# Copies of the k, v and r projections out of PSUM: from ScalarE to VectorE, in an RWKV layer with a gated FFN

## The chip, the cores and the metric

The kernel runs on all 8 cores of one Trainium2 chip. Each core takes one of the 8 sequences of the batch (4096 tokens of 1024 features), with no exchange between cores. The time is device microseconds of the slowest core.

## What is computed

```python
xn = layer_norm(x, ln1_w, ln1_b)
lx = time_shift(xn)
k = (xn * time_mix_k + lx * (1.0 - time_mix_k)) @ w_key
v = (xn * time_mix_v + lx * (1.0 - time_mix_v)) @ w_value
r = (xn * time_mix_r + lx * (1.0 - time_mix_r)) @ w_recept
out = wkv(exp(time_decay), time_first, k, v)      # a scan over the 4096 tokens
x = x + out * sigmoid(r) @ w_output
...
# channel mix: relu(fk)^2 @ f_w_value, gated by sigmoid(fr); then layer norm,
# then silu(x @ wg.T) * (x @ wu.T) @ wd.T with int weights / 127, and layer norm
```

Only the first lines, up to k, v and r, are computed in the part of the program that the change touches.

## The kernel before

The program runs in stages with a barrier of all engines behind each of them: the first computes k, v and r and leaves them in DRAM, the second does the scan, and the later ones do the channel mix and the FFN. The change is in the first stage alone.

That stage is a loop over 8 blocks of 512 tokens, followed by one more call of `emit_projA`. What one turn i emits, in this order:

- SyncE loads the block of x (L406) into one of two buffers.
- The layer norm: VectorE sums (L291, four of 1024 columns), ScalarE sums squares (L297), ScalarE and GpSimd pass small statistics to each other (L301 to L325), and ScalarE applies them (L412).
- TensorE transposes the block in 8 groups (L350). Each group fills a PSUM bank, which ScalarE copies into `xn` (L421).
- VectorE mixes the block with its shifted self: for each of 8 chunks one difference (L427) and three mixes into `m_k`, `m_v`, `m_r` (L434). These have two buffers each, by the parity of i. GpSimd then keeps the last column (L441).
- For i of 1 and more, `emit_projA(i - 1)`: the projections of the block of the turn before. For k, v and r, and for each twice, TensorE does four tiles of 128x512 (L340, 32 matmuls) into four of the 8 PSUM banks, four copies bring them into the four staging tiles of that name (L392), and ScalarE's queue issues four stores of 256 KB to DRAM (L396). Below, k1 and k2 are the first and second group of four of k, and so for v and r.
- GpSimd converts an eighth of the FFN's integer weights with DMAs alone: a load with conversion (L280) and a store (L283), through a single staging tile.

There is no scheduler. Each engine runs its instructions in the order in which the Python emits them, and `Builder.op` adds waits on semaphores from what is read and written. Two of its rules matter. A store names the whole DRAM tensor as what it writes, so each store of `k_fm` waits until the one before has landed. And a group of copies waits until the stores that read the same four staging tiles have landed, which for k2 are those of k1.

Of the kernel before, what the change touches and what calls it, by code (L numbers as in the profile page):

```python
# [9 lines left out]
AF = mybir.ActivationFunctionType  # L10
# [170 lines left out]
def build(debug_phases=99, debug_outs=()):  # L181
# [48 lines left out]
    B = Builder(nc)  # L230
    for s in B.all_sems():
# [17 lines left out]
        reads=[ident], writes=[ident])  # L249
# [4 lines left out]
    for p, h in pv_h.items():  # L254
# [4 lines left out]
         reads=[P["tdec"]], writes=[dw])  # L259
    B.op("scalar", lambda e: e.activation(dw.ap, dw.ap, AF.Exp, scale=-1.0),  # L260
         reads=[dw], writes=[dw])
    B.op("scalar", lambda e: e.activation(eu.ap, P["tfir"].ap, AF.Exp),
         reads=[P["tfir"]], writes=[eu])
# [105 lines left out]
    for w_h, w_sb in ((wk_h, wk_sb), (wv_h, wv_sb), (wr_h, wr_sb)):  # L369
        B.op("gpsimd", lambda e, w_h=w_h, w_sb=w_sb: e.dma_start(  # L370
            w_sb.ap, w_h.rearrange("(c p) o -> p c o", p=128)),
            writes=[w_sb], dma=True)
    B.op("gpsimd", lambda e: e.memset(xn.ap[:, :, 0:1], 0.0), writes=[xn])

    def emit_projA(i):
        t0 = 512 * i
        m_k, m_v, m_r = m_k2[i % 2], m_v2[i % 2], m_r2[i % 2]
        for name, w_sb, m, dst, hb in (("k", wk_sb, m_k, k_fm, HB["k_fm"]),
                                       ("v", wv_sb, m_v, v_fm, HB["v_fm"]),
                                       ("r", wr_sb, m_r, r_fm, HB["r_fm"])):  # L380
            for ob in range(0, DC, 4):
                jobs = []
                for oc in range(ob, ob + 4):
                    pb = pool.take()
                    jobs.append((pb, [w_sb.ap[:, kc, oc * 128:(oc + 1) * 128] for kc in range(DC)],
                                 [m.ap[:, kc, :] for kc in range(DC)]))
                mm_jobs(jobs, 512, [w_sb, m])
                sgs = [stg[name][oc % 4] for oc in range(ob, ob + 4)]

                def evac4(e, jobs=jobs, sgs=sgs):  # L390
                    for k4 in range(4):
                        e.activation(sgs[k4].ap, jobs[k4][0].ap, AF.Copy)  # L392
                    return e.nop()
                B.op("scalar", evac4, reads=[j[0] for j in jobs], writes=sgs)
                for k4, oc in enumerate(range(ob, ob + 4)):
                    B.op("scalar", lambda e, dst=dst, oc=oc, t0=t0, sg_=sgs[k4]: e.dma_start(  # L396
                        dst[oc * 128:(oc + 1) * 128, t0:t0 + 512], sg_.ap),
                        reads=[sgs[k4]], writes=[hb], dma=True)

    if debug_phases >= 1:  # L400
        for i in range(8):
# [6 lines left out]
                writes=[x_t], dma=True)  # L408
# [8 lines left out]
            for dc in range(DC):  # L417
# [7 lines left out]
                    reads=[pb, P["ln1w"], P["ln1b"]], writes=[xn])  # L425
            for dc in range(DC):
# [3 lines left out]
                    reads=[xn], writes=[dnc])  # L430

                def mixes(e, dc=dc, m_k=m_k, m_v=m_v, m_r=m_r):
                    for tm, m in (("tmk", m_k), ("tmv", m_v), ("tmr", m_r)):
# [5 lines left out]
                     reads=[dnc, xn, P["tmk"], P["tmv"], P["tmr"]],  # L439
                     writes=[m_k, m_v, m_r])  # L440
            B.op("gpsimd", lambda e: e.tensor_copy(xn.ap[:, :, 0:1], xn.ap[:, :, 512:513]),  # L441
                 reads=[xn], writes=[xn])
# [23 lines left out]
    if debug_phases >= 2:  # L466
        for j in range(DC):
            kb, vb, rb = kb2[j % 2], vb2[j % 2], rb2[j % 2]
            yb, kmax = yb2[j % 2], kmax2[j % 2]
            for src, hb, b in ((k_fm, HB["k_fm"], kb), (v_fm, HB["v_fm"], vb),  # L470
# [3 lines left out]
                    reads=[hb], writes=[b], dma=True)  # L474
            if j == 7 and "dbg" in debug_outs:
                B.op("sync", lambda e: e.dma_start(dbg_h[:, 0:4096], rb.ap),
                     reads=[rb], dma=True)
# [6 lines left out]
                reads=[kmax], writes=[kmax])  # L484
            B.op("vector", lambda e, kmax=kmax: e.tensor_scalar(
                kmax.ap[:, 1:2], kmax.ap[:, 1:2], 20.0, None, ALU.min),
                reads=[kmax], writes=[kmax])
            B.op("scalar", lambda e, kb=kb, kmax=kmax: e.activation(
                ek.ap, kb.ap, AF.Exp, bias=kmax.ap[:, 1:2]),
                reads=[kb, kmax], writes=[ek])  # L490
            B.op("vector", lambda e, vb=vb: e.scalar_tensor_tensor(
                ekv.ap, ek.ap, 1.0, vb.ap, ALU.mult, ALU.mult),
                reads=[ek, vb], writes=[ekv])
# [3 lines left out]
                reads=[ekv, dw], writes=[Abuf])  # L497
# [3 lines left out]
                reads=[ek, dw], writes=[Bbuf])  # L501
# [3 lines left out]
                reads=[ekv, eu, Abuf], writes=[kb])  # L505
# [3 lines left out]
                reads=[ek, eu, Bbuf], writes=[vb])  # L509
            B.op("vector", lambda e, vb=vb: e.scalar_tensor_tensor(  # L510
                ekv.ap, tmp.ap, 1.0, vb.ap, ALU.add, ALU.mult),
                reads=[tmp, vb], writes=[ekv])
# [4 lines left out]
            if j == 7 and "dbg" in debug_outs:  # L517
                B.op("sync", lambda e: e.dma_start(dbg_h[:, 4096:8192], Abuf.ap[:, 0:4096]),
                     reads=[Abuf], dma=True)
                B.op("sync", lambda e: e.dma_start(dbg_h[:, 8192:12288], kb.ap),  # L520
                     reads=[kb], dma=True)
                B.op("sync", lambda e: e.dma_start(dbg_h[:, 12288:12290], kmax.ap),
                     reads=[kmax], dma=True)
# [5 lines left out]
                reads=[kb, tmp], writes=[yb])  # L529
            B.op("scalar", lambda e, j=j, yb=yb: e.dma_start(  # L530
                y_fm[j * 128:(j + 1) * 128, :], yb.ap),
                reads=[yb], writes=[HB["y_fm"]], dma=True)
# [21 lines left out]
    if debug_phases >= 3:  # L554
        for w_h, w_sb in ((wo_h, wo_sb), (fwk_h, fwk_sb), (fwr_h, fwr_sb)):
            B.op("gpsimd", lambda e, w_h=w_h, w_sb=w_sb: e.dma_start(
                w_sb.ap, w_h.rearrange("(c p) o -> p c o", p=128)),
                writes=[w_sb], dma=True)
# [40 lines left out]
        for i in range(16):  # L599
# [6 lines left out]
                writes=[xc], dma=True)  # L606
            B.op("sync", lambda e, t0=t0, yc=yc: e.dma_start(
                yc.ap, y_fm.rearrange("(c p) t -> p c t", p=128)[:, :, t0:t0 + 256]),
                reads=[HB["y_fm"]], writes=[yc], dma=True)
# [292 lines left out]
```

How the kernel before makes its waits and increments, by code:

```python
    def _wait(self, eng, tok):  # L58
        sem, val, src, flag = tok
        prev = self.waited[eng].get(sem.name, -1)
        if val <= prev:
            return
        self.waited[eng][sem.name] = val
        flag["x"] = True
        self.ops[eng].append(lambda e, s=sem, v=val: e.wait_ge(s.h, v))
# [33 lines left out]
            def fn(e, build=build, sem=sem, step=step):  # L99
                ins = build(e)
                ins.then_inc(sem.h, step)
# [1 line left out]
            def fn(e, build=build, sem=sem, step=step, flag=flag):  # L103
                ins = build(e)
                if flag["x"]:
                    e.drain().then_inc(sem.h, step)
                else:
                    ins.then_inc(sem.h, step)
# [72 lines left out]
def build(debug_phases=99, debug_outs=()):  # L181
# [648 lines left out]
                                 bias=stat.ap[:, 24 + q:25 + q],  # L830
                                 scale=stat.ap[:, 20 + q:21 + q])
                return e.nop()
            B.op("scalar", napplyD, reads=[y2p, stat], writes=[y1tc])
            B.op("sync", lambda e, t0=t0: e.dma_start(
                out_h[t0:t0 + 512, :].rearrange("(q p) d -> p q d", p=128), y1tc.ap),
                reads=[y1tc], dma=True)
    ar.release()
    for ds in B.dsems["sync"] + B.dsems["scalar"]:
        B.raw("sync", lambda e, ds=ds: e.wait_ge(ds.h, ds.n))
    for ds in B.dsems["gpsimd"]:
        B.raw("gpsimd", lambda e, ds=ds: e.wait_ge(ds.h, ds.n))
```

## Time and profile before

| | us |
|---|---|
| two runs of the kernel before | 5155.95 and 5321.26, median 5238.6 |
| the profiled execution's own time | 5163.81 |
| its span, on the slowest core (core 5) | 5162.3 |
| spans of the other cores | 5100.2 to 5147.8 |

The span is from the first instruction to the last on the slowest core, and the time of the execution lies 1.5 us above it. The rows below are of that execution and that core. A row of the timeline gives an instruction's start and duration in us, and in square brackets how long its engine was idle before it and who released it. A merged row (x4) has the duration from the first start to the last end.

### The profile page before, as it was taken

The page shows a single profiled execution, that of the slowest core. Times are in us where ns is not written, and L with a number is a line of the kernel's source. Part 1 is how long each engine was busy: PE and PEld are TensorE (multiplying, and loading weights), DVE is VectorE, ACT ScalarE, POOL GpSimd, SP SyncE. Part 2 cuts the span into 40 slices and gives each one's busy share as a digit, 9 for nine tenths or more (in the row PEclk, how much of TensorE's full clock was granted, in tenths as well). Part 3 has the DMA queues.
Part 4 walks back from the last instruction along what each step waited for, and adds up shares of the span by engine and source line. Part 5 has one row for each costly group of instructions (what it writes and reads, how often), then busy time and mean ns, then how long its engine had stood idle before and what let it go on. Part 6 is the DMA issues. An engine that isn't in the chain of part 4 may idle for free.

```text
span 5162.3 us, 42328 instructions; the slowest of 8 cores (5100.2 to 5162.3 us)
## 1 busy us (share of the span) xinstructions
PE 2882.8 (56%) x14080; PEld 1451.6 (28%) x14080; DVE 1338.4 (26%) x1840; ACT 981.0 (19%) x1414; POOL 145.7 (3%) x328
## 2 busy tenths in 40 slices
PE   0445655400004777777762767764599999155554
PEld 0112222100002444455441323332244444022222
DVE  2222321067742444334430111211011111010101
ACT  1123222122212222232220111121011111011101
POOL 1100000000000000000000000000000000000000
PEclk9966777755556888888886878877799999577777
DMA  6333334533244122221217243233310110413132
GB/s 106 100 108 110 108 100 116 157 143 141 114 94 106 62 82 82 62 82 62 70 50 175 82 135 110 84 128 78 61 66 33 55 44 25 114 57 114 57 114 73
DMA packets 351011, 472.55 MB, mean 92 GB/s; under 512 B 83536, under 2 KB 263760, under 8 KB 345680
## 3 DMA queue, kind: packets, MB, share of 16 engines
q1 hardware_dynamic: 111488, 218.11, 12.8%
q10 hardware_dynamic: 215552, 186.67, 11.1%
q0 software_dynamic: 23760, 65.07, 7.0%
q8 instruction: 119, 1.95, 0.2%
q14 instruction: 92, 0.75, 0.1%
HBM read 293.65 MB, written 203.42 MB: 96 GB/s over the span
## 4 chain that ended last, share of the span: by engine, by line
issue 28%; PEld 20%; DMA 17%; DVE 10%; ACT 7%; DVEq 5%; ACTq 5%; PEldq 4%; another core or an unknown queue 2%; POOLq 1%; POOL 0%; SPq 0%
PEld psum L340 18%; DVEq L106 5%; ACTq L106 4%; PEldq L106 4%; DMA v_fm<-arena 3%; DMA r_fm<-arena 3%; DMA k_fm<-arena 2%; DMA arena<-h_fm 2%; DMA arena<-wd_bf 2%; ACT arena L297 2%; PEld psum L350 2%; POOLq L106 1%; DVE arena L498 1%; DVE arena L494 1%
## 5 line engine op out<-in xcount | busy, mean ns | idle before, releaser
L340 PE MATMUL psum<-arena 128*128 128x512 bf16 (+1 forms) x13312 | 2686.8, 364 | 1548.3 <-DMA arena<-x 529.5
L340 PEld LDWEIGHTS psum<-arena 128*128 128x128 bf16 x13312 | 1333.7, 102 | 2896.5 <-issue 1864.6
L350 PE MATMUL psum<-arena 128*128 128x128 f32 x768 | 196.0, 386 | 702.1 <-ACTq L106 655.7
L297 ACT ACTIVATE arena<-arena 128x1024 f32<-128x1024 f32 x128 | 133.6, 1045 | 1764.7 <-DVEq L106 1487.5
L350 PEld LDWEIGHTS psum<-arena 128*128 128x128 f32 x768 | 117.8, 192 | 784.7 <-issue 784.7
L778 DVE SCALAR_TENSOR_TENSOR arena<-psum,arena 128x512 bf16<-128x512 f32 x192 | 123.7, 686 | 728.3 <-ACTq L106 728.3
L574 DVE TENSOR_SCALAR arena<-psum 128x256 f32<-128x256 f32 x512 | 181.3, 416 | 383.6 <-PEq L106 235.1
L772 ACT ACTIVATE arena<-psum 128x512 bf16<-128x512 f32 x192 | 104.2, 594 | 610.7 <-PEq L106 604.3
L705 DVE SCALAR_TENSOR_TENSOR arena<-psum,arena 128x512 f32<-128x512 f32 x64 | 44.2, 691 | 671.0 <-PEq L106 664.7
L821 DVE SCALAR_TENSOR_TENSOR arena<-psum,arena 128x512 f32<-128x512 f32 x64 | 44.3, 692 | 664.2 <-PEq L106 655.2
L427 DVE SCALAR_TENSOR_TENSOR arena<-arena 128x512 f32<-128x512 f32 x64 | 44.3, 692 | 614.0 <-ACTq L106 602.7
L578 ACT ACTIVATE arena<-arena 128x1024 bf16<-128x1024 f32 x128 | 135.3, 1057 | 334.9 <-DVEq L106 328.9
L392 ACT ACTIVATE arena<-psum 128x512 f32<-128x512 f32 x192 | 99.1, 602 | 517.0 <-DMA v_fm<-arena 163.7
L291 DVE TENSOR_REDUCE arena<-arena 128x1 f32<-128x1024 f32 x128 | 147.9, 1212 | 24.0 <-DMA arena<-x 15.5
L434 DVE SCALAR_TENSOR_TENSOR arena<-arena 128x512 bf16<-128x512 f32 x192 | 132.9, 747 | 15.1 <-DVEq L106 15.1
L652 DVE SCALAR_TENSOR_TENSOR arena<-arena 128x256 f32<-128x256 f32 x128 | 54.5, 426 | 299.9 <-ACTq L106 277.7
L658 DVE SCALAR_TENSOR_TENSOR arena<-arena 128x256 bf16<-128x256 f32 x256 | 112.7, 481 | 25.4 <-DVEq L106 25.4
L513 ACT ACTIVATE arena<-arena 128x4096 f32<-128x4096 f32 x8 | 28.9, 3616 | 292.3 <-DVEq L106 292.3
L311 POOL TENSOR_TENSOR arena<-arena 128x4 f32<-128x4 f32 (+1 forms) x40 | 7.8, 196 | 2678.9 <-ACTq L106 2630.4
L646 ACT ACTIVATE arena<-psum,arena 128x256 f32<-128x256 f32 x128 | 72.4, 565 | 35.3 <-ACTq L106 20.4
L494 DVE TENSOR_TENSOR_SCAN arena<-arena 128x4096 f32<-128x4096 f32 x8 | 69.5, 8693 | 1.6 <-DVEq L106 1.6
L498 DVE TENSOR_TENSOR_SCAN arena<-arena 128x4096 f32<-128x4096 f32 x8 | 69.5, 8693 | 1.0 <-issue 0.2
(75 smaller groups left out, 879.5 us busy)
## 6 DMA issues: line engine op xcount, KB each, us to landing
fk_fm<-arena ACTq DMA_DIRECT2D x16, 2048.0 KB, 8.8
arena<-fk_fm SPq DMA_DIRECT2D x8, 4096.0 KB, 25.1
h_fm<-arena ACTq DMA_DIRECT2D x8, 3072.0 KB, 11.1
arena<-h_fm SPq DMA_DIRECT2D x8, 3072.0 KB, 16.2
arena<-x SPq DMA_DIRECT2D x8, 2048.0 KB, 9.6
k_fm<-arena ACTq DMA_DIRECT2D x64, 256.0 KB, 2.2
v_fm<-arena ACTq DMA_DIRECT2D x64, 256.0 KB, 2.6
r_fm<-arena ACTq DMA_DIRECT2D x64, 256.0 KB, 2.4
```

Of the source, the lines that this page charges most:

```text
L106: e.drain().then_inc(sem.h, step)
L291: e.reduce_sum(stat.ap[:, q:q + 1], xa[:, q, :], AX.X)
L297: e.activation(dump.ap[:, q, :], xa[:, q, :], AF.Square, accum_out=stat.ap[:, 4 + q:5 + q])
L340: last = e.matmul(psumb.ap[:, 0:n], lts[i], rhs[i], start=(i == 0), stop=(i == cnt - 1))
L350: last = e.transpose(bank.ap[:, idx * 128:(idx + 1) * 128], ap, ident.ap)
L434: e.scalar_tensor_tensor(m.ap[:, dc, :], dnc.ap, P[tm].ap[:, dc:dc + 1], xn.ap[:, dc, 0:512], ALU.mult, ALU.add)
L494: B.op("vector", lambda e, j=j: e.tensor_tensor_scan(Abuf.ap[:, 1:4097], dw.ap[:, j:j + 1].to_broadcast([128, 4096]), ekv.ap, 0.0, ALU.mul ...
L498: B.op("vector", lambda e, j=j: e.tensor_tensor_scan(Bbuf.ap[:, 1:4097], dw.ap[:, j:j + 1].to_broadcast([128, 4096]), ek.ap, 0.0, ALU.mult ...
L574: e.tensor_scalar(relu_t.ap[:, k4 * 256:(k4 + 1) * 256], jobs[k4][0].ap[:, 0:256], 0.0, None, ALU.max)
L578: B.op("scalar", lambda e, fb=fb, fkst=fkst: e.activation(fkst.ap[:, fb:fb + 4, :].rearrange("p a b -> p (a b)"), relu_t.ap, AF.Square), r ...
L658: e.scalar_tensor_tensor(m.ap[:, dc, :], dn2.ap, P[tm].ap[:, dc:dc + 1], xn2.ap[:, dc, 0:256], ALU.mult, ALU.add)
L778: e.scalar_tensor_tensor(hbv.ap[:, hc, :], jobs[2 + k2][0].ap, 1.0, sgb.ap[:, hc, :], ALU.mult, ALU.mult)
```

## The change

The four copies of each group are done by VectorE as `tensor_copy`, where ScalarE did them as `activation` with the function Copy. The stores stay in ScalarE's queue, and nothing else is edited.

```diff
@@ -389,9 +389,9 @@
 
                 def evac4(e, jobs=jobs, sgs=sgs):
                     for k4 in range(4):
-                        e.activation(sgs[k4].ap, jobs[k4][0].ap, AF.Copy)
+                        e.tensor_copy(sgs[k4].ap, jobs[k4][0].ap)
                     return e.nop()
-                B.op("scalar", evac4, reads=[j[0] for j in jobs], writes=sgs)
+                B.op("vector", evac4, reads=[j[0] for j in jobs], writes=sgs)
                 for k4, oc in enumerate(range(ob, ob + 4)):
                     B.op("scalar", lambda e, dst=dst, oc=oc, t0=t0, sg_=sgs[k4]: e.dma_start(
                         dst[oc * 128:(oc + 1) * 128, t0:t0 + 512], sg_.ap),
```

VectorE, from the end of the mixes of turn 1 to the first difference of turn 2, in the kernel before (sem_tensor, sem_scalar, sem_vector and sem_gpsimd are the engines' semaphores, d_sync and d_scalar those of DMAs on these queues):

```order
L427 SCALAR_TENSOR_TENSOR arena<-arena 128x512 [waits sem_vector]
L434 SCALAR_TENSOR_TENSOR arena<-arena 128x512 [waits sem_vector]
L434 SCALAR_TENSOR_TENSOR arena<-arena 128x512 x2
L437 NO_OP
L291 TENSOR_REDUCE arena<-arena 128x1 [waits d_sync2,sem_gpsimd]
L291 TENSOR_REDUCE arena<-arena 128x1 x3
```

And at the same place in the changed kernel, up to the first copies of v:

```order
L427 SCALAR_TENSOR_TENSOR arena<-arena 128x512 [waits sem_vector]
L434 SCALAR_TENSOR_TENSOR arena<-arena 128x512 [waits sem_vector]
L434 SCALAR_TENSOR_TENSOR arena<-arena 128x512 x2
L437 NO_OP
L392 COPY arena<-psum 128x512 [waits sem_tensor]
L392 COPY arena<-psum 128x512 x3
L393 NO_OP
L392 COPY arena<-psum 128x512 [waits sem_tensor,sem_vector,d_scalar0,d_scalar1,d_scalar2,d_scalar3]
L392 COPY arena<-psum 128x512 x3
L393 NO_OP
L392 COPY arena<-psum 128x512 [waits sem_tensor]
```

All 24 copies of a turn now stand behind its last mix and ahead of the sums of the next turn (L291). The second group waits for the four stores of the first.

ScalarE at the same turn, from its last copies into `xn` to the first store of v, in the kernel before:

```order
L421 ACTIVATE arena<-psum,arena 128x512 [waits sem_tensor,sem_scalar] x7
L392 ACTIVATE arena<-psum 128x512 [waits sem_tensor]
L392 ACTIVATE arena<-psum 128x512 x3
L393 NO_OP
L396 DMA k_fm<-arena 128x512 [waits sem_scalar]
L396 DMA k_fm<-arena 128x512 [waits d_scalar0]
L396 DMA k_fm<-arena 128x512 [waits d_scalar1]
L396 DMA k_fm<-arena 128x512 [waits d_scalar2]
L392 ACTIVATE arena<-psum 128x512 [waits sem_tensor,d_scalar3]
```

And in the changed kernel:

```order
L421 ACTIVATE arena<-psum,arena 128x512 [waits sem_tensor,sem_scalar] x7
L396 DMA k_fm<-arena 128x512 [waits sem_vector]
L396 DMA k_fm<-arena 128x512 [waits d_scalar0]
L396 DMA k_fm<-arena 128x512 [waits d_scalar1]
L396 DMA k_fm<-arena 128x512 [waits d_scalar2]
L396 DMA k_fm<-arena 128x512 [waits sem_vector,d_scalar3]
L396 DMA k_fm<-arena 128x512 [waits d_scalar4]
L396 DMA k_fm<-arena 128x512 [waits d_scalar5]
L396 DMA k_fm<-arena 128x512 [waits d_scalar6]
L396 DMA v_fm<-arena 128x512 [waits sem_vector]
```

The 24 stores of a turn follow each other in ScalarE's queue, and the first of each group of four waits for VectorE. TensorE's, GpSimd's and SyncE's instructions stand as before.

## Rows read from the trace of the kernel before

**Rows 1.** The page: span, busy time, and the chain that ended last.

```profile
span 5162.3 us, 42328 instructions; the slowest of 8 cores (5100.2 to 5162.3 us)
PE 2882.8 (56%) x14080; PEld 1451.6 (28%) x14080; DVE 1338.4 (26%) x1840; ACT 981.0 (19%) x1414; POOL 145.7 (3%) x328
issue 28%; PEld 20%; DMA 17%; DVE 10%; ACT 7%; DVEq 5%; ACTq 5%; PEldq 4%; another core or an unknown queue 2%; POOLq 1%; POOL 0%; SPq 0%
```

**Rows 2.** Waits, 60 to 1014 us: total us, times, longest us.

```profile
DVE arena L427 <- ACTq L106: 602.7, 8, 80.3
...
ACT arena L392 <- DMA v_fm<-arena: 163.7, 14, 16.1
ACT arena L392 <- DMA k_fm<-arena: 134.0, 14, 13.0
ACT arena L392 <- DMA r_fm<-arena: 113.4, 9, 19.5
...
ACT arena L297 <- DMA r_fm<-arena: 53.4, 6, 12.0
```

**Rows 3.** Timeline of ScalarE and its queue, turn 4.

```profile
512.74 0.78 ACT L421 ACTIVATE arena<-psum,arena 128x512 f32<-128x512 f32 x1 [0.41 <-PEq L106]
...
525.46 6.67 ACTq L396 DMA_DIRECT2D k_fm<-arena  x4
533.99 2.06 ACT L392 ACTIVATE arena<-psum 128x512 f32<-128x512 f32 x4 [8.67 <-DMA k_fm<-arena]
536.19 6.92 ACTq L396 DMA_DIRECT2D k_fm<-arena  x4
543.21 2.07 ACT L392 ACTIVATE arena<-psum 128x512 f32<-128x512 f32 x4 [7.16 <-DMA k_fm<-arena]
545.42 9.33 ACTq L396 DMA_DIRECT2D v_fm<-arena  x4
...
592.21 1.06 ACT L297 ACTIVATE arena<-arena 128x1024 f32<-128x1024 f32 x1 [8.04 <-DMA r_fm<-arena]
```

**Rows 4.** Timeline of VectorE, turn 4 and the start of turn 5.

```profile
513.72 0.69 DVE L427 SCALAR_TENSOR_TENSOR arena<-arena 128x512 f32<-128x512 f32 x1 [78.83 <-ACTq L106]
...
537.07 2.08 DVE L434 SCALAR_TENSOR_TENSOR arena<-arena 128x512 bf16<-128x512 f32 x3 [0.19 <-DVEq L106]
539.40 4.60 DVE L291 TENSOR_REDUCE arena<-arena 128x1 f32<-128x1024 f32 x4 [0.26 <-issue]
617.42 0.69 DVE L427 SCALAR_TENSOR_TENSOR arena<-arena 128x512 f32<-128x512 f32 x1 [73.42 <-ACTq L106]
```

**Rows 5.** Seven windows from first mix to first k1 store; then to last mix's end.

```profile
sum 81.22, DVE 69.00; mean DVE 9.86
...
sum 178.37, DVE 155.05; mean DVE 22.15
```

**Rows 6.** Lines by form, VectorE; then its timeline in the channel mix stage.

```profile
L574 DVE TENSOR_SCALAR arena<-psum 128x256 f32<-128x256 f32 x512 | 181.3, 416 | 383.6 <-PEq L106 235.1 <-ACTq L106 145.3 <-issue 3.2
L434 DVE SCALAR_TENSOR_TENSOR arena<-arena 128x512 bf16<-128x512 f32 x192 | 132.9, 747 | 15.1 <-DVEq L106 15.1
...
L652 DVE SCALAR_TENSOR_TENSOR arena<-arena 128x256 f32<-128x256 f32 x128 | 54.5, 426 | 299.9 <-ACTq L106 277.7 <-DVEq L106 22.2
...
1801.76 1.42 DVE L574 TENSOR_SCALAR arena<-psum 128x256 f32<-128x256 f32 x4 [2.58 <-PEq L106]
```

**Rows 7.** The page's DMA part for 512 to 593 us: 40 slices, GB/s moved.

```profile
GB/s 0 0 0 0 0 0 8 129 129 129 129 0 129 134 133 134 154 243 129 122 129 252 7 114 145 259 110 159 144 235 17 238 104 235 62 125 186 202 159 184
```

**Rows 8.** Timeline of TensorE, turn 4: k2 and r2.

```profile
524.11 7.07 PE L340 MATMUL psum<-arena 128*128 128x512 bf16 x32 [0.97 <-PEq L106]
...
559.84 8.58 PE L340 MATMUL psum<-arena 128*128 128x512 bf16 x32 [6.44 <-ACTq L106]
```

**Rows 9.** Timeline of GpSimd, turn 4: its first and last weight DMA.

```profile
540.45 0.63 POOL L280 DMA_DIRECT2D arena<-wu  x1 [0.65 <-issue]
...
593.12 0.55 POOL L283 DMA_DIRECT2D wu_bf<-arena  x1 [4.16 <-DMA arena<-wu]
```

## The prediction

> **What bounds the kernel now.** I read the page first. No engine is full: TensorE is busy for 56% of the span, VectorE for 26%, ScalarE for 19%, and the chain that ended last is spread over issue, weight loads and DMAs [rows 1]. So shares say nothing here, and the stage that the change touches has to be read by itself. It ends with a barrier, at about 1014 us of the 5162.3 (where the window of [rows 2] ends), and what it gains or loses is passed on whole.
>
> The waits of that stage name the engine that carries it [rows 2]. VectorE waits 602.7 us for ScalarE in 8 waits, one per turn. ScalarE in turn waits for DMAs that its own queue issued: 163.7, 134.0 and 113.4 us ahead of the copies, 53.4 ahead of the next turn's squares, 464.5 us in 43 waits. The bound is ScalarE's queue, in which 24 stores per turn follow each other one landing at a time.
>
> The timeline of turn 4 shows the pattern [rows 3, 4]. I count from S, the start of the first mix on VectorE (513.72). ScalarE ends the last copy into `xn` at 513.52, waits for TensorE's k1, copies it out and issues the first k1 store at S + 11.7 (525.46). Each four stores take three landings to issue (6.67 us for k1). Then come 2.06 us of copies, and so on, until the squares of the next turn at S + 78.5. VectorE mixes meanwhile, without a pause, until 539.15 (537.07 + 2.08), S + 25.4, and then has nothing on the path until the next turn. So two things run side by side in this kernel: 25 us of mixes, and the first copies and stores.
>
> **The change, part by part.** What is new in the order is that k1's copies stand behind the last mix on the same engine.
>
> 1. The first copies of a turn wait for the mixes. In turns 1 to 7, S to the first store is 81.22 us in sum, 11.60 each, and S to the end of the last mix 178.37 in sum, 25.48 each [rows 5]. In the changed kernel the first store can go out 25.48 + 0.20 (a step within VectorE's queue, as the 0.19 in [rows 4]) + the four copies + 0.20 (a handoff between engines: 513.52 to 513.72 in [rows 3, 4]).
>
> No copy of 128x512 on VectorE is in the trace. The nearest row is a TENSOR_SCALAR out of PSUM, f32 to f32, of half the width: 416 ns alone, and 1.42 us for four, so (1.42 - 0.416) / 3 = 0.335 us from start to start [rows 6]. The 256 columns more come at the rate at which VectorE's two widths of one operation differ, 0.69 us for 512 columns [rows 4] and 0.426 for 256 [rows 6], so 1.03 ns each, 0.267 us. That makes 0.602 from start to start, 0.683 for the last, 3 x 0.602 + 0.683 = 2.49 us for four. From below the bound is 1.42 (if the wider copy cost no more than that row), from above 4 x 0.747 = 2.99, the mixes' own duration [rows 6]. I take 2.49.
>
> First store at 25.48 + 0.20 + 2.49 + 0.20 = S + 28.37 in place of S + 11.60: +16.77 us, times 7 turns = +117.4. In the tail, projections of block 7, no mix stands ahead.
>
> 2. The second group of each name (k2, v2, r2, 24 in all) still waits for the four stores of the first, as its staging tiles are theirs. It was 2.06 us of copies and 0.14 to the store (536.19 - 533.99 = 2.20 [rows 3]) and becomes 2.49 + 0.20 = 2.69: +0.49, times 24 = +11.8.
>
> 3. The first groups of v and r (16), and k1 of the tail (1), lose their place on ScalarE. From the issue of k2's fourth store to v1's first there are now 545.42 - (536.19 + 6.92) = 2.31 us [rows 3]. In the changed kernel VectorE copies v1 out during k2's stores, and v1's first store can go at once, while k2's fourth is still on its way. I take 2.1 for a gain of 2.31, with 0.2 for two stores in flight: 17 x 2.1 = -35.7. The bounds are 2.31 and 0, should the two merely share the DMA engines.
>
> The rate speaks for nearly all of it: while k1's stores land alone 129 GB/s are moved, and where a weight DMA runs beside a store the sum reaches 243 to 259 [rows 7].
>
> The Trainium skill says of a DMA issued by GpSimd (DMA: Bandwidth & Descriptors, Anatomy of one DMA) that about 2.0 us of it are fixed, most of that the receipt of the last write. By that rule two in flight overlap almost wholly, and term 3 would be its full -39.3. The trace agrees in kind only: by the page's figures a store of 256 KB would take an estimated 2.6 us, and k1's here take 6.67 / 3, about 2.2, with their issue [rows 3].
>
> 4. What could be late next. The sums of the next turn (L291, 4.60 us [rows 4]) move behind r2's copies. The squares follow three landings after r2's first store, and start 8.04 us after r2's copies [rows 3], so about 3 us are left and the sums cost nothing. TensorE gets its banks later: v1's matmuls can start once k1 is copied, at S + 28.2. At 7.07 to 8.58 us a group [rows 8] v1 is done by S + 37, and its copies stand behind k2's, which start about S + 37. The weight DMAs on GpSimd start behind the last mix in both kernels and take 53 us [rows 9]: they end at S + 80, before the next statistics at about S + 97. Of the stores' time (S + 12 to S + 78) the last 51 us lay beside them. It will be S + 28 to S + 92, and the first 52 us lie beside them, so the contention hardly changes. I cost these at nothing. The next turn's S follows the squares as before.
>
> The sum: 117.4 + 11.8 - 35.7 = +93.5 us on the execution's own 5163.8: 5257.3, or 1.8% more. This execution is near the lower of the two runs shown (5155.95). The median of the two, 5238.6, lies 75 us above it and is a mean with the high run, so I don't add to it.
>
> One rule goes against the new engine. The half-width row shows no faster mode: 335 ns from start to start for 256 columns, 1.3 ns each with what one instruction costs [rows 6]. The Trainium skill (VectorE: DVE Perf Modes, Why PSUM operands drop a tier) says that a copy of 32-bit data takes two per cycle between SBUF tiles, but one if an operand lies in PSUM; the trace agrees. By the page's cycle table, PSUM to SBUF, four copies would be an estimated 2.63 us, and by two per cycle about 1.6; with the 31 groups that are waited for (7 + 24) that is 4 us more in the sum, or 28 less.
>
> **The rivals.**
>
> Rival A, the loss is larger (slower by over 2%). Two stores in flight share the DMA engines, and term 3 shrinks to 0.5 x 17 = -8.5: 5163.8 + 117.4 + 11.8 - 8.5 = 5284.5. The slices of 129 and 259 GB/s [rows 7] speak against it. It could also come by TensorE, which now pauses 10.7 us ahead of v1 (k2 ends at 531.18, S + 17.5 [rows 8]). If its groups then took twice 7.07, v1, v2, r1 and r2 would end at S + 28.2 + 56.6 = S + 84.8. R2's copies, now at 582.10 or S + 68.4 (592.21 - 8.04 - 2.07 [rows 3]), would be due at 68.4 + 16.8 + 2 x 0.49 - 2 x 2.1 = S + 82.0, so 2.8 us late, and 7 x 2.8 = 20 us more give 5277. R2's group, which followed a pause of 6.44, took 8.58, not 14 [rows 8]. It decides from 10 us above the forecast on.
>
> Rival B, the stores get shorter (not slower). All 43 waits for stores come to 464.5 us [rows 2]; undisturbed, as in k1 and k2 of turn 4, they would be about 24 x 8.67 + 19 x 7.16 = 344 [rows 3]. If the later start took the stores out of the weight DMAs' way, up to 120 us would go: 5257 - 120 = 5137, no slower than before. It decides from 94 us of relief on. But the stores only move with the mixes' end, and the weight DMAs start at that same point [rows 9], so I see no more than noise.
>
> Rival C, the copies are quick. If four cost 1.42 us, 31 groups save 1.07 each: 33 us, 5224. The half-width row [rows 6] speaks against it.
>
> **How the numbers follow.** Forecast with its small errors, between 5230 and 5267: 0.58. Rival A with its two causes: 0.31. Rival C: 0.08. Rival B: 0.03. A measurement of this kernel tells about 2% from no change, so the border is 5267 above and 5061 below. Slower by over 2%: rival A, 0.31. Within 2%: 0.68. Faster by over 2%: 0.01, as even rival B with all its relief doesn't get there. The range takes the bounds of the unknown terms: below, copies of 1.42 and the full 2.31: 5257 - 33 - 4 = 5220; above, copies of 2.99 (31 x 0.50 = 15.5) and no gain in term 3 (35.7): 5308.
>
> **What would show each step.** In the changed profile the first k1 store of turns 1 to 7 should stand 28 us behind the first mix, with copies of about 0.68 us, four in 2.5. The turn should be about 14 us longer and the stage's end, now 1014, near 1107. ScalarE should wait for VectorE once per turn for about 15 us (S to the first store), and v1's and r1's first stores should follow the fourth of the group ahead within 0.5 us. TensorE should stand idle some 10 us before v1. The later stages should be as they were. I am wrong if the first store comes before the mixes end, if the stores' landings differ in the mean by over 0.3 us from now, or if a later stage changes by over 20 us.

## The result, and the profile after

The changed kernel is slower by 2.1%: the ratio of its runs to those of the kernel before is 1.0212, with a 95% interval of 1.0179 to 1.0244. The median is 5283.91 us of 11 runs, against 5175.17 of 10. These medians hold runs in which one die's cores had a lower clock; the ratio leaves those out on both sides. The profiled execution took 5272.66 us, 108.9 more than that of the kernel before (5163.81). The forecast was 5257, +1.8%, with a range of 5220 to 5308. The measured difference is just above the border of 2%, and the interval reaches across it, so whether the loss is over or under 2% stays open; that there is one does not.

The page of the changed kernel, the span, what each engine did, and the group of the copies:

```profile
span 5271.1 us, 42491 instructions; the slowest of 8 cores (5222.0 to 5271.1 us)
...
PE 2891.7 (55%) x14080; PEld 1452.8 (28%) x14080; DVE 1458.3 (28%) x2032; ACT 881.9 (17%) x1222; POOL 145.6 (3%) x328
...
L392 DVE COPY arena<-psum 128x512 f32<-128x512 f32 x192 | 119.2, 683 | 426.9 <-DMA v_fm<-arena 160.1
```

Against [rows 1], ScalarE did 99 us less and VectorE 120 us more. No sum of busy time tells that the kernel lost 109 us by it. A copy takes 683 ns on VectorE in the mean, as forecast.

The timeline of turn 4 on ScalarE and its queue, core 3, answers to [rows 3]:

```profile
547.30 0.78 ACT L421 ACTIVATE arena<-psum,arena 128x512 f32<-128x512 f32 x1 [0.21 <-ACTq L106]
576.66 22.89 ACTq L396 DMA_DIRECT2D k_fm<-arena  x8
599.64 26.67 ACTq L396 DMA_DIRECT2D v_fm<-arena  x8
626.39 20.66 ACTq L396 DMA_DIRECT2D r_fm<-arena  x8
647.21 1.06 ACT L297 ACTIVATE arena<-arena 128x1024 f32<-128x1024 f32 x1 [99.12 <-DMA r_fm<-arena]
```

ScalarE ends its last copy into `xn` at 548.08 and computes nothing for 99 us. For the first 28.6 us of that its queue issues nothing either. The first store is 28.45 us behind the first mix (548.21), where it was 11.74. From there on the stores of one tensor follow those of the other with no gap: the row of k ends at 576.66 + 22.89 = 599.55, and the first v store goes out at 599.64.

The same turn on VectorE answers to [rows 4]:

```profile
548.21 0.69 DVE L427 SCALAR_TENSOR_TENSOR arena<-arena 128x512 f32<-128x512 f32 x1 [27.27 <-ACTq L106]
...
571.52 2.08 DVE L434 SCALAR_TENSOR_TENSOR arena<-arena 128x512 bf16<-128x512 f32 x3 [0.19 <-DVEq L106]
574.06 2.49 DVE L392 COPY arena<-psum 128x512 f32<-128x512 f32 x4 [0.46 <-issue]
588.27 2.48 DVE L392 COPY arena<-psum 128x512 f32<-128x512 f32 x4 [11.72 <-DMA k_fm<-arena]
591.22 2.48 DVE L392 COPY arena<-psum 128x512 f32<-128x512 f32 x4 [0.46 <-issue]
614.10 2.48 DVE L392 COPY arena<-psum 128x512 f32<-128x512 f32 x4 [20.40 <-DMA v_fm<-arena]
...
637.56 2.48 DVE L392 COPY arena<-psum 128x512 f32<-128x512 f32 x4 [18.04 <-DMA r_fm<-arena]
640.30 4.60 DVE L291 TENSOR_REDUCE arena<-arena 128x1 f32<-128x1024 f32 x4 [0.25 <-issue]
```

The copies of k1 start 0.46 us after the last mix. Those of v1 (591.22) come straight behind those of k2, and v1's staging tiles are full at 593.70, 6 us before v's first store. The sums of the next turn end at 644.90, ahead of the squares at 647.21, so they cost nothing.

TensorE in the same turn, core 3, answers to [rows 8]:

```profile
555.36 7.07 PE L340 MATMUL psum<-arena 128*128 128x512 bf16 x32 [0.97 <-PEq L106]
576.73 9.04 PE L340 MATMUL psum<-arena 128*128 128x512 bf16 x32 [14.30 <-DVEq L106]
590.93 8.75 PE L340 MATMUL psum<-arena 128*128 128x512 bf16 x32 [5.17 <-DVEq L106]
```

After k2 it waits 14.30 us until VectorE has emptied k1's banks. V1 is then done at 585.77, before its copies start at 591.22, so the wait costs nothing here.

The seven windows from first mix to first store, as in [rows 5], now for core 3:

```profile
sum 197.06, DVE 172.49; mean DVE 24.64
```

That is 28.15 us each, and it is 28.14 to 28.16 on all eight cores. In the kernel before it was 11.60 on core 5, whose rows the forecast used, but between 10.12 and 11.60 over the cores, 10.71 in the mean. Core 5 was the longest of the eight.

To see where the time went I add up each part over the turns, mean over 8 cores. Block 7 has no turn of mixes behind it; its stores are the tail.

| us | before | after | difference in sum |
|---|---|---|---|
| first mix to first store, 7 turns | 10.71 | 28.15 | +122.1 |
| first to last store's issue, 7 turns | 72.64 | 72.83 | +1.3 |
| last store's issue to next first mix, 6 | 26.13 | 25.79 | -2.0 |
| tail (block 7), with the step into it | 73.8 | 62.0 | -11.8 |
| end of the first stage | 997.2 | 1107.1 | +109.9 |
| all that follows | 4132.6 | 4141.9 | +9.3 |

The stage holds the difference. The rest moved 9 us, and over the two kernels and the three of the next section that keep the weights where they were it lies between 4132 and 4159 us, so that is noise. The end of the stage has a standard deviation over the 8 cores of 11.8 us before and 6.2 after, which leaves the 109.9 uncertain by some 5 us.

The last thing to see is how long a store takes to land. The chain of waits, core 5, turn 4: first the kernel before, where v1's first store is the row at 545.42.

```profile
545.42 2.05 DMA v_fm<-arena
547.53 4.06 DMA v_fm<-arena
551.66 2.70 DMA v_fm<-arena
554.43 3.10 DMA v_fm<-arena
```

Then the changed kernel, where it is the row at 603.86. The two rows ahead are k1's last store and k2's first.

```profile
588.44 3.12 DMA k_fm<-arena
594.30 2.34 DMA k_fm<-arena
...
603.86 5.09 DMA v_fm<-arena
609.01 3.07 DMA v_fm<-arena
612.15 4.59 DMA v_fm<-arena
```

This pair is an extreme one. Over blocks 0 to 5 and the 8 cores v1's first store lands in 4.06 us where it was 3.14, and r1's in 3.75 where it was 2.57. The stores that have a weight DMA beside them land in 2.99 us (18.8 of 24 per turn) where it was 2.85 (18.3 of 24). Nearly all of that rise lies in v1's and r1's first stores: without these two it is 2.88 where it was 2.85. The stores with no weight DMA beside them take 2.10 where they took 2.13.

### The profile page after: what moved, and what is told of

Read it like the earlier page. It is cut to its first block, busy times and chain, and to the rows that moved or that the text cites. A ratio compares the mean times of both kernels' runs of the same rounds, so it can differ in the third digit from the quotient of the medians.

```text
span 5271.1 us, 42491 instructions; the slowest of 8 cores (5222.0 to 5271.1 us)
## 1 busy us (share of the span) xinstructions
PE 2891.7 (55%) x14080; PEld 1452.8 (28%) x14080; DVE 1458.3 (28%) x2032; ACT 881.9 (17%) x1222; POOL 145.6 (3%) x328
## 4 chain that ended last, share of the span: by engine, by line
issue 26%; PEld 19%; DMA 18%; DVE 12%; DVEq 8%; ACT 6%; ACTq 4%; PEldq 4%; another core or an unknown queue 2%; POOLq 1%; POOL 0%; SPq 0%
PEld psum L340 17%; DVEq L106 7%; ACTq L106 4%; DMA v_fm<-arena 3%; DMA k_fm<-arena 3%; PEldq L106 3%; DMA r_fm<-arena 3%; DMA arena<-h_fm 2%; DMA arena<-wd_bf 2%; ACT arena L297 2%; PEld psum L350 1%; POOLq L106 1%; DVE arena L498 1%; DVE arena L494 1%
## 5 line engine op out<-in xcount | busy, mean ns | idle before, releaser
L392 DVE COPY arena<-psum 128x512 f32<-128x512 f32 x192 | 119.2, 683 | 426.9 <-DMA v_fm<-arena 160.1
L291 DVE TENSOR_REDUCE arena<-arena 128x1 f32<-128x1024 f32 x128 | 147.9, 1212 | 19.5 <-DMA arena<-x 10.7
L434 DVE SCALAR_TENSOR_TENSOR arena<-arena 128x512 bf16<-128x512 f32 x192 | 132.9, 748 | 12.7 <-DVEq L106 12.7
L311 POOL TENSOR_TENSOR arena<-arena 128x4 f32<-128x4 f32 (+1 forms) x40 | 7.8, 196 | 2769.6 <-ACTq L106 2722.8
L513 ACT ACTIVATE arena<-arena 128x4096 f32<-128x4096 f32 x8 | 28.9, 3616 | 291.9 <-DVEq L106 291.9
L478 ACT ACTIVATE arena<-arena 128x4096 f32<-128x4096 f32 x8 | 28.9, 3616 | 251.7 <-DMA arena<-r_fm 214.5
L494 DVE TENSOR_TENSOR_SCAN arena<-arena 128x4096 f32<-128x4096 f32 x8 | 69.5, 8693 | 1.6 <-DVEq L106 1.6
```

The lines of the kernel that those rows point to most:

```text
L291: e.reduce_sum(stat.ap[:, q:q + 1], xa[:, q, :], AX.X)
L392: e.tensor_copy(sgs[k4].ap, jobs[k4][0].ap)
L434: e.scalar_tensor_tensor(m.ap[:, dc, :], dnc.ap, P[tm].ap[:, dc:dc + 1], xn.ap[:, dc, 0:512], ALU.mult, ALU.add)
L494: B.op("vector", lambda e, j=j: e.tensor_tensor_scan(Abuf.ap[:, 1:4097], dw.ap[:, j:j + 1].to_broadcast([128, 4096]), ekv.ap, 0.0, ALU.mul ...
```

## The experiments

Eleven kernels were run. The end of the first stage is the last landing of a k, v or r store, the mean over the 8 cores of one profile. Its standard deviation over the cores is 2 to 17 us, called scatter below; how far it would differ between executions was not measured. The change of the whole kernel by each experiment is the ratio to the kernel before.

### Only v1 and r1 on VectorE

```diff
+                on_v = name != "k" and ob == 0
...
-                        e.activation(sgs[k4].ap, jobs[k4][0].ap, AF.Copy)
+                        if on_v:
+                            e.tensor_copy(sgs[k4].ap, jobs[k4][0].ap)
+                        else:
+                            e.activation(sgs[k4].ap, jobs[k4][0].ap, AF.Copy)
...
-                B.op("scalar", evac4, reads=[j[0] for j in jobs], writes=sgs)
+                B.op("vector" if on_v else "scalar", evac4,
+                     reads=[j[0] for j in jobs], writes=sgs)
```

> The kernel before, with only the first copies of v and of r (v1, r1) on VectorE; k1, k2, v2, r2 stay on ScalarE. This is term 3 of the prediction alone. My term as predicted: 2.1 us gained 16 times, 34 us, ratio to before 0.993, end of the first stage (mean over cores, 997 us in the kernel before) at 963. Theory now (the first store of v and of r lands later because the one ahead is still in flight, as 4.06 and 3.75 us after the change against 3.14 and 2.57 before it): 2.31 less about 1.05 gained, 20 us, stage end at 977. Rival, the two stores merely share the DMA engines: nothing gained, stage end at 997.

Measured: ratio 0.9962 (0.9925 to 0.9999), stage end at 986.0 us, 11 us less than before. The ratio stands for 20 us less, with an interval from nothing to 39, so it can't tell the forecast's 34 from a small gain. The profile shows 11, uncertain by 5, between the 20 of the theory and the nothing of the rival. First to last store's issue took 71.13 us a turn, 1.5 less than 72.64, where 2 x 2.1 was forecast. A store landed in 2.92 us in the mean instead of 2.81.

### k back on ScalarE

The same edit with `on_v = name != "k"`: all copies of v and r on VectorE, those of k on ScalarE.

> The changed kernel with k's copies (k1, k2) back on ScalarE, v's and r's on VectorE. Theory (what costs is that the first copies stand behind the mixes, 17.5 us a turn): the first store comes again 10.7 us after the first mix, and the stage ends at about 997 - 20 (v1, r1 hidden) + 7 (v2, r2 slower by 0.46 each) = 984 us, ratio to before 0.997. Rival, VectorE's copies are dear wherever they stand (their duration, the handoff, more contention): two thirds of the 110 us stay, stage end at 1070, ratio 1.014.

Measured: ratio 1.0005 (0.9967 to 1.0044), stage end at 990.9 us. First mix to first store is 10.97 us again. With 16 of the 24 copies of a turn still on VectorE, the stage ends 116 us earlier than in the changed kernel and 6 earlier than in the one before, and the ratio shows no difference to the latter. So for v and r neither the engine nor its copies' duration costs anything that can be measured. What cost was where k's copies stood.

### k1 and k2 in between the mixes

```diff
                      writes=[m_k, m_v, m_r])
+                if i >= 1 and dc == 2:
+                    emit_projA(i - 1, (0,))
+                if i >= 1 and dc == 5:
+                    emit_projA(i - 1, (1,))
...
             if i >= 1:
-                emit_projA(i - 1)
+                emit_projA(i - 1, (2, 3, 4, 5))
```

> The changed kernel, all copies on VectorE, with k1's copies placed behind the third of the eight chunks of mixes and k2's behind the sixth. Theory: first store about 12.8 us after the first mix (28.15 in the changed kernel, 10.7 before), 15.3 us less in each of 7 turns, and the stage ends near 1107 - 107 = 1000 us, ratio to before about 1.001. Rival, ScalarE's queue needs the copies' engine for another reason than order: the stage stays above 1070 us, ratio 1.014 or more.

Measured: ratio 1.0034 (0.9997 to 1.0071), stage end at 1016.7 us, 90 less than the changed kernel. First mix to first store is 12.37 us (12.8 expected). All copies are on VectorE here, as in the changed kernel; only their place differs. The stage ended 17 us later than expected. Part of that is the tail: from block 7's first store to the end it took 70.6 us, and 61.6 in the changed kernel. The last weight DMA is issued 22 us after block 7's first store here, and 8 us before it in the changed kernel, so they run beside it again.

### Without weight DMAs beside the stores

Three kernels in which GpSimd's weight conversion is moved whole into the scan stage: the kernel before, the one with v1 and r1 on VectorE, and the changed one.

```diff
-            emit_ffn_dequant(i / 8.0, (i + 1) / 8.0)
...
+    wstg = [ar.bf16([128, 3072], "wstg0")] * 2
...
     if debug_phases >= 2:
+        emit_ffn_dequant(0.0, 1.0)
         for j in range(DC):
```

> The kernel before with the conversion of the FFN's weights moved whole from the first stage to the scan stage, so that no DMA of GpSimd runs beside the stores of k, v, r. It is the base for the next two. Theory (stores land in 2.81 us in the mean because weight DMAs run beside them, in about 2.18 without them, as in the tail): 192 x 0.63 = 121 us less, the first stage ends at 876 us (mean over cores) in place of 997. If the landings are slow for another reason, it stays near 997.

> The same with v1's and r1's copies on VectorE: term 3 without weight DMAs. Theory (the gain of 2.31 is eaten by weight DMAs that fill the gaps, not by the second store in flight): 2.1 gained 16 times, the first stage 34 us shorter than in the run before it. Rival (two stores in flight share the engines in any case): 11 us shorter, as with the weight DMAs beside them (997.2 to 986.0).

> The changed kernel with the weight conversion moved to the scan stage. Theory: against the first of these three kernels +122 (first copies behind the mixes, 17.45 x 7) + 11 (k2, v2, r2) - 36 (17 x 2.1) = 97 us, near the 93.5 of the prediction. Rival (sharing in any case): 110 us or more, as with the weight DMAs beside them.

Measured, with the time between the first and the last store's issue of a turn, and the mean landing of a store:

| | stage end | against the first | first to last issue | landing |
|---|---|---|---|---|
| kernel before, weights later | 854.5 | | 60.53 | 2.23 |
| v1, r1 on VectorE, weights later | 828.8 | -25.7 | 57.54 | 2.28 |
| changed kernel, weights later | 944.7 | +90.2 | 56.61 | 2.22 |

The first kernel's stage came out 22 us shorter than expected: 41 of its 143 us lie in turn 1, whose first mix starts at 141.6 us in place of 183.1, since its statistics no longer stand behind turn 0's weight DMAs; the shorter landings, 2.23 us in place of 2.81, are enough for the rest.

The change costs 90 us here (97 expected by the theory, 110 or more by the rival) and 110 with the weight DMAs in place. Between the first and last store it now gains 3.9 us a turn (60.53 to 56.61), where with them it lost 0.2. V1 and r1 alone give 26 us, where they gave 11; that lies between the 34 of the theory and the 11 of the rival. The scatters of 10 to 16 us over the cores leave these differences uncertain by 7 to 8 us each, and those with the weight DMAs in place by 5. So the step from 11 to 26 us is within the noise, and that from 110 to 90 just outside of it. What is clear is the stretch between first and last store of the whole change: a gain of 3.9 us a turn, uncertain by 0.8, against a loss of 0.2, uncertain by 0.7. Without weight DMAs the gain is what was forecast or more, and with them it is gone. First mix to first store is 28.15 and 10.96, nearly as with the weight DMAs (28.15 and 10.71). The ratio of the second kernel was 0.9951 (0.9826 to 1.0077); the third has none, as it was run twice.

As a change to the kernel, moving the weights gains nothing (0.9971, 0.9906 to 1.0036): the stage is 143 us shorter and the rest 136 us longer (4269.0 for 4132.6). The scan stage then loads k, v and r beside them; that this is what makes it longer was not tested.

### The stores no longer wait for each other

```diff
-                        reads=[sgs[k4]], writes=[hb], dma=True)
+                        reads=[sgs[k4]], dma=True)
```

> The kernel before with its stores of k, v and r no longer waiting for each other (they write different parts of the tensors; staging tiles and the barrier still guard them). Theory: the bound moves from ScalarE's queue to GpSimd's, where the weight DMAs of a turn (57 us) start behind the last mix and the next statistics stand behind them: a turn of 25.7 + 57 + 20 = 103 us in place of 109.5, and the first stage ends at about 925 us (997 now).

> The changed kernel with the stores unchained in the same way. Theory (the change costs what it does because the stores' chain starts with the first copies; the weight DMAs start behind the mixes in both): within 15 us of the run before it. If the first copies behind the mixes cost by themselves, it is some 110 us longer than that one.

Measured: the first has a ratio of 0.9842 (0.9794 to 0.9891) and its stage ends at 911.4 us; the second's stage ends at 932.5, 21 later in place of 110. It was expected within 15, and 21 is a little more. From first mix to first mix a turn is only 1.2 us longer, 7 us in six turns, as the 17.3 us ahead of the first store are taken out of a wait; the other 14 come in turn 7 and block 7, where nothing hides them. The second has no ratio, as it was run twice. The timeline of GpSimd in the first of them, core 3, shows the wait:

```profile
564.47 0.53 POOL L280 DMA_DIRECT2D arena<-wu  x1 [2.31 <-DMA wu_bf<-arena]
568.83 0.54 POOL L283 DMA_DIRECT2D wu_bf<-arena  x1 [3.83 <-DMA arena<-wu]
569.39 0.21 POOL L311 TENSOR_TENSOR arena<-arena 128x4 f32<-128x4 f32 x1
```

The statistics of the next turn (L311) start 0.02 us behind the last weight DMA's issue, without any wait: they had stood behind it. That weight chain starts at the end of the mixes in both kernels, so where it sets the turn, the change is nearly free.

### Both edits, with the copies on either engine

The stores unchained and the weights moved to the scan stage, with ScalarE's copies and with VectorE's.

> The kernel before with the stores unchained and the weight conversion moved to the scan stage. Theory: TensorE's six groups bound the turn, about 77 us in place of 109.5; the first stage ends at about 704 us, the rest takes 4269 us as when the weights alone were moved: 4973 us, ratio to before 0.965.

> The changed kernel with the same two edits. Theory: copies stand behind the mixes again, and now TensorE waits for the banks until 28 us after the first mix: a turn of about 90 us, the first stage ends near 795 us, 90 longer than in the run before it, ratio to before 0.983. Rival (VectorE's copies relieve ScalarE once stores don't wait): as fast as that one or faster.

Measured: with ScalarE 0.9614 (0.9585 to 0.9644), stage end at 690.4 us; with VectorE 0.9886 (0.9805 to 0.9967), stage end at 806.2 us. The change costs 116 us in this frame, 26 more than expected, and by the wait that was expected, not by the stores' chain. TensorE in the second, core 6:

```profile
326.58 7.07 PE L340 MATMUL psum<-arena 128*128 128x512 bf16 x32 [1.00 <-ACTq L106]
334.62 7.07 PE L340 MATMUL psum<-arena 128*128 128x512 bf16 x32 [0.98 <-PEq L106]
355.19 9.29 PE L340 MATMUL psum<-arena 128*128 128x512 bf16 x32 [13.50 <-DVEq L106]
```

K1 and k2 run, then v1 waits 13.5 us for VectorE to empty k1's banks, behind the mixes. In the changed kernel itself that wait (14.30 us) is there too, and hidden behind the stores' chain. A turn is 17.0 us longer here (74.99 to 91.98 from first mix to first mix), the whole delay of the first copies.

### The weights behind the statistics

Stores unchained, copies on ScalarE, and:

```diff
             ln_stats(x_t, 4, stat, n_t)
+            emit_ffn_dequant(i / 8.0, (i + 1) / 8.0)
...
-            emit_ffn_dequant(i / 8.0, (i + 1) / 8.0)
```

> The kernel before, copies on ScalarE, stores unchained, and the weight DMAs of a turn issued by GpSimd right behind that turn's statistics (ahead of the last-column copy L441) in place of behind the mixes. Theory: the weight stream of 57 us then fits beside TensorE's and ScalarE's work of a turn, the turn stays near the 75 us of the kernel with the weights in the scan stage, and the scan stage is not lengthened: first stage at about 720 us, the rest 4140 us, 4860 us in all, ratio to before 0.942. If the weight stream still holds the next statistics back, the first stage stays above 850 us.

Measured: ratio 0.9462 (0.942 to 0.9504), the stage ends at 715.0 us and the rest takes 4138.7. This beats both kernels, by 5.4% and about 7.3%. GpSimd's timeline, core 6:

```profile
353.73 0.55 POOL L283 DMA_DIRECT2D wu_bf<-arena  x1 [3.95 <-DMA arena<-wu]
354.79 0.20 POOL L442 COPY arena<-arena 128x8 f32<-128x8 f32 x1 [0.51 <-issue]
366.43 0.20 POOL L311 TENSOR_TENSOR arena<-arena 128x4 f32<-128x4 f32 x1 [11.44 <-ACTq L106]
```

The last weight DMA of a turn is issued 12.7 us ahead of the next statistics, which now wait for ScalarE (11.44 us) and not for the weights.

## Why the prediction was right, and where its sum was off

**Where the time fell.** The profiled execution took 5272.66 us, 15 more than the sum. That is inside the range of 5220 to 5308, but 6 us above the band of 5230 to 5267 which the forecast held most likely (0.58), in the stretch that it had given to rival A (0.31). The direction and the mechanism were right; the size was near.

**The mechanism and its place.** The forecast was that the first copies, behind the mixes on VectorE, hold the stores back for the length of the mixes, and that only that matters. The timeline shows it, and two experiments make it more than a reading: k's copies back on ScalarE return all of the loss, with two thirds of the copies still on VectorE, and the same copies on VectorE placed between the mixes return 90 of 110 us.

**Term 1 (117.4).** Measured 122.1. The new distance was 28.15 for 28.37, right to 0.2 us. The old one was taken from core 5, the slowest of the profile, where it was 11.60; the mean is 10.71. That is 6.2 us in 7 turns, less the 1.5 of the other error. A core that is slowest in one execution is not a typical one: its stage ended at 1014, the mean at 997. It is luck that the forecast end of 1107 is the measured mean to the digit, 1107.1: the forecast added its 93.5 to core 5's 1014. On core 5 itself the stage ended at 1109.5, 95.5 later; over the cores it was 109.9 later in the mean.

**Term 2 (+11.8).** The step from landing to next store was +0.49 in the forecast. On core 5 of the changed kernel it is 594.30 - (588.44 + 3.12) = 2.74 us from the landing of k1's fourth store to the issue of k2's first. In the kernel before it was 536.19 - 533.91 = 2.28 on that core. That is +0.46. Right. From the fourth issue of a group to the next one's first, mean over cores and turns, the three steps of a turn grew by 1.65 us together, for 1.47 forecast.

**Term 3 (-35.7), the step that failed in size.** With term 2 in it, the forecast for a turn's stores was 3 x 0.49 - 2 x 2.1 = -2.7 us. Measured: +0.2, so 20 us of gain are missing over 7 turns. The 23 steps from one store's issue to the next, mean over 7 turns and 8 cores, show where:

| us a turn | before | after | forecast | measured | without weight DMAs |
|---|---|---|---|---|---|
| last store of k2 to first of v1, of v2 to r1 | 5.27 | 0.83 | -4.6 | -4.44 | -4.44 |
| first store of v1 and of r1 to their second | 6.32 | 8.34 | +0.4 | +2.02 | +0.29 |
| into k2, v2, r2 | 15.21 | 16.86 | +1.5 | +1.65 | +0.99 |
| the other 16 steps | 45.85 | 46.81 | 0 | +0.96 | -0.76 |
| first to last | 72.64 | 72.83 | -2.7 | +0.2 | -3.9 |

The gaps did go, as forecast. What was mis-sized is the 0.2 us for two stores in flight. The first store of v1 and of r1, issued 0.41 us behind the one ahead, cost 1.0 us each where weight DMAs ran beside it, and 0.15 where none did. That is 11 of the 20 us. The other 16 steps make 7 more, where part 4 had put the contention at no change. A store with a weight DMA beside it takes 0.9 us more than one without (3.04 and 2.17 us over all 7 turns of the kernel before), and 19.2 stores a turn have one where 18.4 had: by that an estimated 0.7 us a turn.

So it was rival A's sharing in a weaker form: each gap brought 1.2 us, where the forecast had 2.1 and rival A 0.5. The weight DMAs have to be there for it, as the last column shows, and a store in flight alone is not enough. They themselves did not change: one landed in 3.65 us before and 3.66 after, and those of a turn took 58.3 and 58.5 us. Where the stores lose is less sure than that they do. In the kernels with v1 and r1, or all of v and r, on VectorE the first stores of v1 and r1 lost 1.0 and 1.1 us a turn and the other 16 steps 2.5 and 1.8. Why a second store in flight is dear beside weight DMAs alone, no run here tells.

**The tail.** Forecast -4.8 (3 x 0.49 - 3 x 2.1), measured -11.8. Block 7 used to start while the last weight DMAs still ran. In the kernel before, core 5, its first store and the last weight store:

```profile
943.63 10.55 ACTq L396 DMA_DIRECT2D k_fm<-arena  x4
951.59 0.54 POOL L283 DMA_DIRECT2D wd_bf<-arena  x1 [7.57 <-DMA arena<-wd]
```

In the changed kernel, core 3, GpSimd's last weight DMAs are issued before block 7's first store, which goes out at 1048.15:

```profile
1030.20 0.53 POOL L280 DMA_DIRECT2D arena<-wd  x1 [5.72 <-DMA wd_bf<-arena]
1038.40 0.54 POOL L283 DMA_DIRECT2D wd_bf<-arena  x1 [7.67 <-DMA arena<-wd]
```

That they are gone gives back about 7 us. The kernels with the weights later bear it out: without weight DMAs the tail takes 65.9 us before the change (73.8 with them) and 62.5 after it, -3.4.

**The sum** was 93.5 for 109.9 in the stage: +6 from the core's choice, -1.5 from the new distance, +20 from term 3, -7 from the tail, -2 from the step between a turn's last store and the next first mix. The errors went both ways and cancelled in part; that the sum came within 16 us owes something to that. Part 4's other claims held: the sums of the next turn ended 2.3 us before they were needed (3 expected), TensorE's wait ahead of v1 was hidden (14.30 us for 10.7 forecast; k2's matmuls ended 14 us after S, not 17.5, and v1's began at S + 28.5), and later stages did not move beyond noise. From first mix to first mix a turn is 16.6 us longer where 14 were forecast, mostly by the missing gain of term 3. One sign was misread: ScalarE was to wait for VectorE for about 15 us before a turn's first store, and by the forecast's own first store at S + 28 it had to be 28, which it was (28.6).

**The Trainium skill.** The Trainium skill's rule that 32-bit copies out of PSUM go at one per cycle (VectorE: DVE Perf Modes, Why PSUM operands drop a tier) agrees with the trace: 683 ns for 512 columns, four in 2.49 us. The estimate by the page's cycle table for one per cycle was 2.63, for two per cycle 1.6. The Trainium skill's rule on a DMA's fixed 2 us (DMA: Bandwidth & Descriptors, Anatomy of one DMA) would have given the full -39.3 in term 3. By these runs that would nearly have held without weight DMAs, where the second store in flight cost 0.15 us; beside them it cost 1.0, and there the measurement decides. Its figures give an estimated 2.6 us for a store of 256 KB; with no weight DMA beside it a store from ScalarE's queue landed in 2.1.

**The rivals.** B (shorter stores) and C (quick copies) did not occur: the mean landing went up, from 2.81 to 2.88 us, and four copies took 2.49. Of A's two causes, sharing is there in part; TensorE did not matter, since its groups after the pause took 9.04 and 8.75 us and not twice 7.07.

## What to carry to other kernels

Moving work to an idle engine costs what stands ahead of it in that engine's order, not what the engine's busy share suggests. Before such a move, list for each moved instruction what it waits for and when that is ready, and compare with when its new neighbour ahead is done: here k1's tiles were ready 9.5 us after the first mix on core 5 (8.5 in the mean over the cores), and the last mix ended after 25.5. If the engine is to change all the same, move those pieces whose inputs come late (v1, r1), or place them between the neighbours.

Read the wait behind the wait. ScalarE's 19% of busy time hid a queue that stood at DMA landings, and one word, the tensor named in `writes`, chained them. Taking it away and giving the next statistics precedence over bulk DMAs on GpSimd was worth 5.4%, more than any choice of engine for the copies.

When a gap in a chain of DMAs is closed, the first transfer behind it flies beside the last one ahead. Price that with whatever else moves at the time: here it took 1.0 of 2.2 us beside a third stream, and 0.15 without one.

## What the runs showed that I had not expected

Closing two gaps of 2.2 us a turn brought 3.9 us without weight DMAs beside the stores (with the slower second groups already in it), and nothing measurable with them. The weight DMAs took the same time in both kernels, 3.65 and 3.66 us each, so the stores bore the whole of it.

The same change cost 110, 90, 21 and 116 us in four frames of the first stage: stores chained, with and without weight DMAs; stores unchained with GpSimd as the bound; and unchained with TensorE as the bound. In the third the delay was hidden by a queue that started at the same point in both, and in the fourth it came back as a wait for PSUM banks.
